# Experts' products as three products of high and low parts, with weights split ahead of time and read through a ring of four experts

## What is computed

```python
xn = layernorm(x)
scores = sigmoid(xn @ gate_w.T)                  # 32 experts, 8 chosen per token (2 of 4 groups)
cw = chosen scores, normalised, times 2.5        # weight of each token and expert
x_lat = xn @ fc1_w.T                             # 256 wide
h = relu(einsum('tl,eil->eti', x_lat, w1))**2    # 256 -> 256, per expert
h = h * cw.T[:, :, None]
y_lat = einsum('eti,eli->tl', h, w2)             # 256 -> 256, per expert, summed over experts
routed = y_lat @ fc2_w.T
shared = relu(xn @ shared_up_w.T)**2 @ shared_down_w.T
out = x + attention(xn) + shared + routed
```

## Time and profile before

| | |
|---|---|
| median of 3 runs | 1973.32 us |
| the profiled execution: its own time, its span | 1969.18 us, 1967.6 us |
| PE busy over the span | 1762.7 us, 90% |
| DVE, ACT, POOL busy | 1150.8, 902.4, 828.3 us |
| first and last addition of a tile (POOL, line 1340) | starts at 1185.3 and 1898.8 us |
| loads of the experts' weights | 64 of 256 KB |
| granted clock of PE, mean over the span | 0.969 of 2.4 GHz |

### The profile page before, as it was taken

One profiled execution on the slowest core, in us unless ns is written; L12 is line 12 of the kernel. 1 busy time (PEld: TensorE's weight loads), 2 busy tenths in 40 slices (PEclk: granted clock), 3 DMA queues, 4 the chain that ended last, 5 costly groups with the idle time before them and its releaser, 6 DMA issues. The chain is left out here.

```text
span 1967.6 us, 40451 instructions
## 1 busy us (share of the span) xinstructions
PE 1762.7 (90%) x10144; PEld 1357.3 (69%) x10145; DVE 1150.8 (58%) x3350; ACT 902.4 (46%) x2474; POOL 828.3 (42%) x704
## 2 busy tenths in 40 slices
PE   5802899999999999999999987799999999999978
PEld 5801676777867677776877755577777777777756
DVE  7687776767767677685767842233333333333337
ACT  2320674756747577574765732233333333333321
POOL 0051242433434334342343404566666666666640
PEclk9955899999999999999999999999999999999989
DMA  7883343433344334443343439877777777777779
GB/s 289 340 326 42 92 124 110 137 108 113 117 122 134 110 111 130 120 130 95 118 134 114 126 115 283 209 117 123 126 125 119 125 126 117 117 114 115 118 166 356
DMA packets 190791, 285.97 MB, mean 145 GB/s; under 512 B 30022, under 2 KB 132558, under 8 KB 187442
## 3 DMA queue, kind: packets, MB, share of 16 engines
q0 software_dynamic: 60528, 96.90, 25.7%
q1 hardware_dynamic: 75058, 121.97, 20.2%
q10 hardware_dynamic: 55088, 65.67, 11.4%
HBM read 128.07 MB, written 134.14 MB: 133 GB/s over the span
## 5 line engine op out<-in xcount | busy, mean ns | idle before, releaser
L1340 POOL DMA_INDIRECT sums<-e_y,e_row x288 | 447.3, 1553 | 311.4 <-DVE e_y L1296 138.5
L720 POOL DMA_INDIRECT slot_rows<-m_row,m_idx x256 | 263.8, 1031 | 525.1 <-ACT m_sc L772 444.0
L772 ACT ACTIVATE m_sc<-m_sc,m_low 128x512 f32<-128x512 f32 (+3 forms) x512 | 283.9, 556 | 147.7 <-DVE m_low L901 146.6
L1369 PE MATMUL e_psH<-e_w,e_xt 128*128 x1152 | 323.2, 403 | 0.2
L1369 PE MATMUL e_psY<-e_w,e_ht 128*128 x1152 | 299.0, 382 | 0.0
L901 DVE CUSTOM_DVE_ANT_0 m_sc<-m_psS,cst 128x512 f32<-128x512 f32 (+3 forms) x512 | 230.2, 486 | 104.7 <-PE m_psS L1053 104.4
L1296 DVE TENSOR_SCALAR e_y<-e_psY,e_row 128x256 f32<-128x256 f32 x288 | 139.4, 484 | 237.4 <-DMA sums<-e_y,e_row 123.3
L1289 DVE TENSOR_SCALAR e_relu<-e_psH 128x256 f32<-128x256 f32 x288 | 122.3, 425 | 227.9 <-PE e_psH L1369 227.9
L1252 ACT ACTIVATE e_xt<-e_psX 128x256 f32<-128x256 f32 x288 | 110.7, 384 | 273.5 <-PE e_psX L1358 273.5
L1369 PEld LDWEIGHTS e_psH<-e_w,e_xt 128*128 128x128 f32 x1152 | 196.1, 190 | 41.6 <-issue 1.2
L1257 ACT ACTIVATE e_ht<-e_psT 128x256 f32<-128x256 f32 x288 | 110.6, 384 | 239.6 <-PE e_psT L1383 228.7
(11 more groups left out here) (186 smaller groups left out, 3104.7 us busy)
## 6 DMA issues: line engine op xcount, KB each, us to landing
e_row<-slot_rows ACTq DMA_DIRECT2D x288, 144.5 KB, 2.3
m_qs<-m_qhi SPq DMA_DIRECT2D x264, 64.0 KB, 2.0
e_w<-in_w SPq DMA_DIRECT2D x64, 256.0 KB, 4.0
m_qs<-m_qlo SPq DMA_DIRECT2D x132, 64.0 KB, 2.0
f_xt<-in_x SPq DMA_DIRECT2D x8, 1024.0 KB, 9.3
xnt_hi<-f_hi SPq DMA_DIRECT2D x8, 1024.0 KB, 4.3
xnt_lo<-f_lo SPq DMA_DIRECT2D x8, 1024.0 KB, 7.8
sums<-empty POOLq DMA_DIRECT2D x32, 256.0 KB, 2.8
```

The lines of the kernel that those rows point to most:

```text
L720: pool.indirect_dma_start(out=xs, out_offset=bass.IndirectOffsetOnAxis(ap=idx[u][:, k:k + 1], axis=0), in_=row[u][:, :], in_offset=None).t ...
L772: nc.scalar.activation(cols, cols, ACT.Exp, bias=low[:, h % 2, i:i + 1], scale=-1.0, accum_out=total[:, h % 2, i:i + 1]).then_inc(exp_done, 1)
L1340: pool.indirect_dma_start(out=sums[u % 2], out_offset=bass.IndirectOffsetOnAxis(ap=row[u % NR][:, ROW - 1:ROW].bitcast(U32), axis=0), in_= ...
L1369: mm = pe.matmul(out[u % 2][:, 0:INTER], lhs[u % 2][:, c * P:(c + 1) * P], w[:, bass.ds(e * W + c * INTER, INTER)], start=(c == 0), stop=( ...
```

## The change

1. The experts' weights are split into high and low parts. In each of the 128 first steps of `middle` (16 per batch) SP loads 128 x 256 values into `m_split`, ACT copies them to their high part, DVE subtracts to get the low part, and SP writes both to `parts` in memory: 1 MB per expert. To make room, `m_sq` and `m_qlo` go (their results are written in place) and `m_row` has one buffer.
2. In `experts` the products are `three` in place of plain fp32. Weights lie in a ring of four experts (`e_w`, 1 MB each); SP loads an expert's 1 MB when the last tile of the expert four before is through. The table also holds each tile's ring slot and each expert's last tile. PE reads the slot for each product (`find_slot`) and, in `hidden`, the expert too, to wait for its weights.
3. ACT writes high parts of x and h and does the scaling of the rows (`weigh`); DVE writes the low parts, relu and the square.
4. POOL's subtractions in `routing` are cut into pieces of 512 columns. DVE has two more linked instructions at the end of `routing`, and the tables are three DMAs.
5. Of the 32 groups' attention and shared results, 16 in place of 10 are loaded before the last stage; loads in it are six in place of five ahead.

```diff
@@ routing
             for k, (dram, hi, lo, n) in enumerate(pieces):
                 pool.wait_ge(hi_made, k + 1)
-                nc.gpsimd.tensor_tensor(lo, stage[:, k % R, 0:n], hi.bitcast(F32), ALU.subtract).then_inc(lo_made, 1)
+                for a in range(0, n, S):
+                    part = slice(a, a + S)
+                    last = nc.gpsimd.tensor_tensor(lo[:, part], stage[:, k % R, part], hi[:, part].bitcast(F32), ALU.subtract)
+                last.then_inc(lo_made, 1)
@@ middle, ACT and DVE
+                def split_high(s):
+                    act.wait_ge(split_moved[s % 3], moved(b, s, 1))
+                    nc.scalar.activation(split[s % 3][:, 0, :], split[s % 3][:, 1, :].bitcast(F32), ACT.Copy).then_inc(split_hi, 1)
+                def split_low(s):
+                    dve.wait_ge(split_hi, b * NH + s + 1)
+                    nc.vector.tensor_tensor(split[s % 3][:, 1, :], split[s % 3][:, 1, :].bitcast(F32),
+                                            split[s % 3][:, 0, :].bitcast(F32), ALU.subtract).then_inc(split_lo, 1)
                     if s < NH:
                         mask_and_min(s, ROWS[2])
                         mask_and_min(s, ROWS[3])
+                    if 1 <= s <= NH:
+                        split_low(s - 1)
@@ experts, SP
+            for k in range(RING, E):
+                arrived(k - 1)
+                end = sp.value_load(table[0:1, 6 * P + k - RING:6 * P + k - RING + 1], min_val=1, max_val=SLOT_TILES)
+                sp.wait_ge(y_done, end + BASE)
+                load(k)
+                if k >= E - NP:
+                    g = k - (E - NP)
+                    sp.dma_start(part[g], partial[g * P:(g + 1) * P, :]).then_inc(early_in, 16)
@@ experts, PE
-            def load_expert(i, u):
-                expert[u % NR] = pe.value_load(table[0:1, bass.ds(i * NR + u, 1)], min_val=0, max_val=E - 1)
-
-            def product(i, u, w, out, lhs, done):
-                e = expert[u % NR]
+            def find_slot(i, u):
+                slot[u % NR] = pe.value_load(table[0:1, bass.ds(i * NR + (3 * P + u), 1)], min_val=0, max_val=RING - 1)
+
+            def product(i, u, m, out, lhs, done):
+                at_ = slot[u % NR] * W
                 for c in range(LC):
-                    mm = pe.matmul(out[u % 2][:, 0:INTER], lhs[u % 2][:, c * P:(c + 1) * P],
-                                   w[:, bass.ds(e * W + c * INTER, INTER)], start=(c == 0), stop=(c == LC - 1))
+                    tok = slice(c * P, (c + 1) * P)
+                    rhs = (w_sb[:, bass.ds(at_ + (2 * (LC * m + c) + k) * PIECE, PIECE)] for k in range(2))
+                    mm = three(pe, out[u % 2][:, 0:PIECE], [a[u % 2][:, tok] for a in lhs], rhs, c == 0, c == LC - 1)
                 mm.then_inc(done, 1)
 
             def hidden(i, u):
 
-                pe.wait_ge(xt_made, num(i, u, 1))
-                pe.wait_ge(w_ready, expert[u % NR] + 1)
-                product(i, u, w1_sb, psH, xt, h_done)
+                pe.wait_ge(xlo_made, num(i, u, 1))
+                expert = pe.value_load(table[0:1, bass.ds(i * NR + u, 1)], min_val=0, max_val=E - 1)
+                pe.wait_ge(w_ready, expert + 1)
+                product(i, u, 0, psH, (xhi, xlo), h_done)
@@ experts, ACT
+            def weigh(i, u):
+                e = act.value_load(table[0:1, bass.ds(i * NR + u, 1)], min_val=0, max_val=E - 1)
+                act.wait_ge(y_done, num(i, u, 1))
+                if not first(i, u, NY):
+                    act.wait_ge(added[u % 2], sums_done(i, u - NY))
+                nc.scalar.activation(y[u % NY][:, :], psY[u % 2][:, 0:LAT], ACT.Copy,
+                                     scale=row[u % NR][:, bass.ds(e + LAT, 1)]).then_inc(y_made, 1)
```

More of the change, by code:

```diff
@@ L40 @@
 BASE = 16
-WIDTHS = dict(ident=P, tri=P, mask=S, cosq=S, sinq=S, cosk=S, sink=S, token=G, earlier=NG * NG, tile=3, lane=1, spare=1)
+WIDTHS = dict(ident=P, mask=S, cosq=S, sinq=S, cosk=S, sink=S, tri=P, token=G, earlier=NG * NG, tile=3, lane=1, spare=1)
 COL, _at = {}, 0
@@ L48 @@
 NCONST = _at
+NKEPT = COL["tri"].start
+RCOL = {_n: slice(_c.start - NKEPT, _c.stop - NKEPT) for _n, _c in COL.items() if _c.start >= NKEPT}
+RING = 4
+NTABLE = 2 * 3 * P + E
+PIECE = 256
 def at(i, per, n):
@@ L599, in middle @@
         bp = sb("m_bp", [P, D])
-        row = [sb(f"m_row{u}", [P, ROW]) for u in range(2)]
+        row = sb("m_row", [P, ROW])
         idx = [sb(f"m_idx{u}", [P, TOPK], U32) for u in range(2)]
         pidx = sb("m_pidx", [P, E // (G // 2)], U32)
+        split = [sb(f"m_split{u}", [P, 2, PIECE], F32R) for u in range(3)]
         psS = [pb(f"m_psS{i}") for i in range(2)]
@@ L624, in middle @@
         saved = sem("m_saved")
-        row_in = [sem(f"m_row_in{u}") for u in range(2)]
+        row_in = sem("m_row_in")
         idx_made = [sem(f"m_idx_made{u}") for u in range(2)]
@@ L630, in middle, with moved @@
         pidx_made = sem("m_pidx_made")
+        split_hi, split_lo = sem("m_split_hi"), sem("m_split_lo")
+        split_moved = [sem(f"m_split_moved{u}") for u in range(3)]
         block = ctx.enter_context(nc.Block())
+        def moved(b, s, n):
+            return b * (32 * len(range(s % 3, NH, 3))) + (16 * BASE + 32 * (s // 3) + 16 * n)
         NQ = 3 * 16
@@ L687, in _ @@
                 sp.wait_ge(landed, value)
+            for u in range(3):
+                sp.wait_ge(split_moved[u], moved(B, u, 0))
         @block.gpsimd
@@ L819, in batch @@
                         ta(t, 2)
+                    if s < NH:
+                        split_high(s)
                     if s in Q_AT:
@@ L1137, with experts @@
 NY = 4
-WR = 2
-NP, RC = 10, 5
-def experts(nc, w1, w2, fc2, cst, experts_dram, xs, sums, partial, out):
+NP, RC = 16, 6
+def experts(nc, parts, fc2, cst, experts_dram, xs, sums, partial, out):
     with ExitStack() as ctx:
@@ L1391, in _ @@
-            pipeline(pe, ((1, load_expert), (0, turn_x), (1, hidden), (3, load_expert), (2, turn_h), (3, result)),
+                product(i, u, 1, psY, (hhi, hlo), y_done)
+            pipeline(pe, ((1, find_slot), (0, turn_x), (1, hidden), (3, find_slot), (2, turn_h), (3, result)),
                      SLOT_TILES // NR, NR)
```

256 lines of the change are left out of this document (143 added, 113 removed).

## The result

The changed kernel takes 2396.3 us (median of 4 runs, 2391.6 to 2397.3) against 1972.3 (median of 4, 1969.4 to 1979.6): ratio 1.2141, 95% interval [1.2108, 1.2174]. The prediction was 2345 us, with a range of 2250 to 2435.

What follows compares the result with a forecast made beforehand. PE's instruction queue was taken to bound a tile in `experts`, the array just below. 1969 + 377 + 5 + 8 - 13 - 5 = 2341 us, plus 4 for the median: 2345 us, range 2250 to 2435.

Steps and rivals of the forecast that it cites:

- The queue as the mechanism: In `experts`, PE's instruction queue, with a third reading and more address instructions, sets the step: 3.8 us a tile.
- Its size: In `experts`, first to last addition: 2.41 + 0.8 + 0.5 + 0.1 = 3.8 us a tile, +377 us (+291 to +434).
- The loads of 1 MB per nine tiles wait for nobody: In `experts`, at 3.8 us a tile, weight loads (one in 34 us) and the additions' chain (2.3) cause no waiting.
- The queue is the bound today, with the array just below: In `experts` before the change, PE's queue sums to the whole 2.41 us step; the array needs about 2.3.
- `middle`, +8: In `middle`, DVE's subtractions and ACT's copies mostly hide in existing waits, extra issues and traffic cost nothing: +8 us.
- `routing` -13: In `routing`, POOL's quarter pieces cut DVE's waiting from some 20 us to 6: -13 us (-18 to 0).
- start +5: Start of `experts`: row loads wait for the table, the first product for 1 MB: +5 us (2 to 8).
- last stage -5: Last stage: six groups of 256 KB fewer to read, 1.5 MB at 345 GB/s: -5 us (-6 to 0).
- A: In `experts`, queue cost is hidden, array and additions decide: 2.3 us a tile before loads' cost, 1959 us; chance 0.09.
- B: In `experts`, part of the queue's cost is overlapped: 3.2 us a tile, about 2170 us; chance 0.10.
- C: In `experts`, PE's clock falls to 1.2 GHz: 4.2 us a tile, about 2460 us; chance 0.08.
- D: `middle` pays in full and DVE becomes its bound: +54 in place of +8, about 2390 us; chance 0.08.

Runs made afterwards that it cites:

- rows_ahead: Changed kernel with ACT's copies and weighing three half-steps later, so rows load about three tiles earlier: 2304.9 us.
- one_rows_ahead: Changed kernel with one table reading a tile on PE (18 for 16 tiles) and rows loaded earlier: 2052.8 us, ratio 1.040 to the kernel before.
- fixed_slots: Changed kernel with the edits of rows_ahead and no_loads, and ring slots given by tile number, so eight address instructions a tile go: 2044.1 us.
- unmoved: Changed kernel with `middle`'s weight fetches and writes left out, ACT's copies and DVE's subtractions kept on three pieces loaded once: 2378.7 us.
- unsplit: Changed kernel with ACT's copies and DVE's subtractions in `middle` left out, each piece fetched and written twice unsplit: 2378.4 us.
- no_loads: Changed kernel loading only the first four experts' weights, the other 28 loads of 1 MB left out: 2310.3 us.

## Why the prediction was right, and where it wasn't

- **The queue as the mechanism: right.** Three readings a tile, matmuls 0.12 us apart, idle time put down to "issue", POOL waiting for ACT. Against rows_ahead, one_rows_ahead shortens only PE's list and gives back 252 us between first and last addition; fixed_slots gives back 269 (it has no loads either; in the last 47 tiles, without loads in both, the step falls by 0.90 us all the same). One argument for it misreads the rows: the weight loads start right behind a reading, but "never a stored matmul in between" is not so. `hidden`'s four matmuls start from 1300.03 us on, 0.22 apart, and run on to 1300.99, while PE's queue has been at the next reading since 1300.2. Matmuls were stored and covered part of each reading; by its records the array stood still less than 8 us of 590.
- **Its size: too large by 59 us.** Without late rows the step is 3.60 us, not 3.8: +318 in place of +377. The third reading, taken at 0.8 us a tile, takes 0.75 of the queue (0.64 net of the longer address instructions that replaced it; 0.55 to 0.59 in the fp32 kernel, where the queue had some slack); four more address instructions, 0.5 us, measure 0.45 to 0.47; the four bare matmuls, 0.1, nothing. And the 2.41 us they were added to were not all the queue's: its own sum was about 0.1 less.
- **"The loads of 1 MB per nine tiles wait for nobody": wrong, 85 us.** POOL's chain was looked at and the loads' own deadline; what else is on the DMA queues during a load, ACT's rows of 144 KB with two tiles of lead, was not. That and the first error cancel by luck, so +404 looks nearer to +377 than its parts are.
- **"The queue is the bound today, with the array just below": half right.** Adding a reading costs 0.6 us at once; taking nearly one out gives nothing. Queue, array and additions were within about 0.1 us of each other, and the queue was not the highest of the three.
- **`middle`, +8: too small.** It paid 29.6 us in the profiled execution, about 23 in the mean of eight. The sum took DVE's and ACT's work as nearly hidden, where unmoved shows some 10 us for it, and put the moving of the pieces, 256 issues and 48 MB, at nothing, where unsplit shows some 12.
- **`routing` -13, start +5, last stage -5:** -10.2, +7.6, -3.3. In `routing` DVE's long instructions became short, as forecast. At the start the first expert's 1 MB was there at 1195.9 us and the first row, issued at 1192.0 behind it, only at 1198.9: PE waited for the row and not for the weights, the same late rows as later on. The last stage was not taken apart.
- **Rivals:** A and B are out, since the step followed the queue's sum, each reading and address at nearly its full price. C, the clock, was half there: mostly at waits of some us for a row, and in rows_ahead in 14 short stretches without such waits, while in the changed kernel it is 1.00 from 2178.9 to 2329.1 at the full 3.58 us. It did not set the step: rows_ahead runs at 3.61 us with 14 falls, no_loads at 3.60 with 5. D's price for `middle`, 54 us, was less than half real (23).

## What to carry to other kernels

Count a tile's instructions on PE's own queue before its passes through the array: with a table read at run time, each reading (0.75 us here) and each computed address (0.12 us) is paid in full once the matmuls are short, and fewer array cycles then buy nothing. When a load is made larger, look at the smallest lead of any transfer that shares the memory with it, not at the load's own deadline. When a bound is removed and nothing is gained, the next one was level with it: add work as well as remove it, since only the two together show how close they are. And before two halves of a loss are set against the whole, look at how much the same stretch varies where its code is the same: here 12 us of 985.

## What was not expected of the hardware

- PE's granted clock was 0.50 at the end of a single wait of 4.6 us and stayed there for some 4.7 us of work. With PE idle for over a quarter of every step of 3.6 us it stayed at 1.00 for 150 us at the end of the changed kernel's tiles, but fell 14 times in rows_ahead, behind a wait of 0.9 us for the queue.
- A row of 144 KB that takes 2.4 us landed after 7.7 us when issued 0.34 us behind a load of 1 MB.
- A computed address on a matmul costs PE's queue 0.11 to 0.12 us, a matmul without one nothing that shows; a reading of the table with its register instructions costs it 0.75 us.
